# Graph step and expert layer on one core: weighted edge rows split into two fp32r parts, and nine node groups computed ahead instead of seven

## The chip, the cores and the metric

The kernel runs on one core of one Trainium2 chip. The metric is device time of one launch in microseconds (us), the median of several executions; less is better. The core has five engines with a queue each: TensorE (PE), VectorE (DVE), ScalarE (ACT), GpSimd (POOL) and SyncE (SP).

## The reference, cut to what matters

```python
def gnn(X, src, dst, w, W, b):                      # 12500 nodes x 256, 200000 edges, dst sorted
    support = X @ W
    return segment_sum(support[src] * w[:, None], dst, 12500) + b

def ffn(x, ...):                                    # 8 experts, 256 -> 512 -> 256
    rw = softmax(softmax(mean(x) @ Wr + br) * scale)        # one routing for all nodes
    top_w, top_i = top_k(rw, 2); top_w = softmax(top_w)
    y = sum(top_w[k] * (gelu(x @ W1[top_i[k]] + b1) @ W2[top_i[k]] + b2) for k in (0, 1))
    return layernorm(y + x) * gamma + beta

x = x + gnn(layernorm(x), src, dst, edge_weight, W, b)
x = x + ffn(layernorm(x))
```

The two experts are known only when the mean over all nodes is known, that is after the whole graph step.

## The kernel before, in words

**Data.** Nodes lie in 98 tiles of 128 (NT), which stand in 25 groups of four (NG, GT). Edges lie in 1564 columns of 128 (NE), called slots here; they are worked off backwards, so that the first node tiles have about 8 slots each and the last one 158.

**Opening, about 145 us.** Tables are built that say where each node tile ends in the list of slots. Each node row times its 1/deviation is written to `xr_d`. The first 96 slots (FRESH) are gathered from `x` itself, and VectorE works out their weights.

**Edge stage, to about 1994 us.** For each slot GpSimd issues an indirect DMA (line 513) that gathers 128 rows of 256 into `G`, a ring of 64 (RING). VectorE makes a weighted one-hot `OH` (line 969; ring of 8, OHR): 1 times the edge weight where the edge's destination is the row of the node tile. TensorE adds `OH.T @ G` into PSUM bank 0 (`edge`, line 1255), in fp32. After every second slot `event` (line 1257) looks whether something is due. What is due stands in an order written at build time by `events()` and turned into slot numbers on the chip:

- END: a node tile is complete. `chores` (line 1205: transposes, the product with W, more transposes, for this tile and those before it) and then `begin` (line 1221), which starts the next tile with the two slots that may hold edges of both tiles, matched by `OHX`. ScalarE does the `section` (line 652) of the tile: `copy`, `across`, `x1_row`, `pre`, `square`, `match` for the tile after the next, `root`, `turned`, `normal`.
- UPS, BOTH, DOWNS: a unit of expert work. The first 7 groups (AHEAD) go through all 8 experts before the routing is known, in fp32: `unit_up` (line 1227) and `unit_down` (line 1237). These are 56 units (UNITS); their results go to `y_d`. A BOTH event is the down products of one unit and the up products of the next. `events()` spreads them from tile 18 on by `room`, a weight per tile worked out from its slots.

**Post stage, from about 2010 us.** The routing is worked out. Then for each of the 18 groups that were not computed ahead (`post`) TensorE runs the two chosen experts as three fp32r products each (high x high, low x high, high x low): eight steps of `up` (line 1302) and `down` (line 1319), where step i of `up` for group k+1 stands before step i of `down` for group k. VectorE goes through one iteration per k: eight times `low_h` (line 1084, the low part of the hidden rows), and between them `total` and `give` (lines 1086, 1117: the sum, the layer norm) of group k-2, `low` (line 1050) of group k+1, and, if k-2 is in `pre_of`, `total` and `give` of one group computed ahead as well. `pre_of` = {1 + (len(post) - 3) * a // AHEAD}: with 7 groups ahead that is k-2 in 1, 3, 5, 7, 9, 11, 13, every second iteration. GpSimd adds beta to each group's rows (line 524), B2 to those of a group computed ahead (line 522), and works out the 1/deviation (line 529). SyncE's queue holds, in the order of the groups: the load of `YL` three groups on, a wait until the group is finished (`s_fin`), its store, the next loads. So the load behind a group computed ahead waits until that one is finished:

```python
            for n, g in enumerate(order):
                m = len(tiles(g))
                if g >= AHEAD:
                    if k + 3 < len(post):
                        load_yl(k + 3)
                    k += 1
                e.wait_ge(s_fin, 4 * n + m)
```

ScalarE makes the high part `YTh` from `YL` in `high` (line 747), in step 3 of the iteration before the one that uses it, and the activations of `hidden` (lines 794, 797) stand behind it in its queue.

Of the kernel before, what the change touches and what calls it, by code (L numbers as in the profile page):

```python
# [4 lines left out]
P = 128  # L5
NODES, D, F, E = 12500, 256, 512, 8
# [6 lines left out]
RING, GS, OHR = 64, 16, 8  # L13
# [8 lines left out]
AHEAD = 7  # L22
# [52 lines left out]
assert 2 * NEV <= 512  # L75


def gnn_ffn(nc, x, dflat, srct, dstt, wt, W, b, Wr, br, W1, b1t, W2, b2, gamma, beta, cst, iota_e, evt, out):
# [13 lines left out]
    with ctx:  # L92
# [14 lines left out]
        g_bc, be_bc, B2 = sb("g_bc", [P, D]), sb("be_bc", [P, D]), sb("B2", [P, D])  # L107
# [15 lines left out]
        b1s, b2s = sb("b1s", [P, 2, 4]), sb("b2s", [P, 2, D])  # L123
# [6 lines left out]
        ARENA = 49152  # L130
# [20 lines left out]
        G, OH = early("G", [P, RING, D]), early("OH", [P, OHR, P])  # L151
        Wsb = early("Wsb", [P, 2, D])
        BB, Bh, Bl, b2r = early("BB", [P, D]), early("Bh", [P, D], f32r), early("Bl", [P, D], f32r), early("b2r", [P, D], f32r)
        OHX, OHT = early("OHX", [P, 2, P]), early("OHT", [P, 2, 2, P])
# [10 lines left out]
        YE = early("YE", [P, 2, GT * D])  # L165
        XS = At(w_at)("XS", [P, XBUF, GT, D])
        Gf = G[:, :, :].rearrange("p r d -> p (r d)")

# [26 lines left out]
        W1A = At(4 * ARENA - 4 * E * 2 * F)("W1A", [P, E, 2, F])  # L195
# [11 lines left out]
        assert late.at - 4 * HID * GT * P <= 4 * ARENA - 4 * E * 2 * F  # L207
        YP = At(w2s_at)("YP0", [P, 2, GT, D]), late("YP1", [P, 2, GT, D])
        Z = late("Z", [P, 3, GT, D])

# [16 lines left out]
        s_bn, s_aggr, s_pow, s_oh = sem("dve_bn"), sem("dve_aggr"), sem("dve_pow"), sem("dve_oh")  # L227
# [94 lines left out]
        def _(e):  # L322
# [100 lines left out]
            e.dma_start(g_bc[:, :], row(gamma).to_broadcast([P, D])).then_inc(gb_in, 16)  # L423
            e.dma_start(be_bc[:, :], row(beta).to_broadcast([P, D])).then_inc(gb_in, 16)
# [24 lines left out]
            for k in range(2):  # L449
                e.dma_start(W2s[:, k, :, :], W2[bass.ds(chosen[k], 1), :, :].rearrange("o (c p) n -> p (o c) n", p=P)).then_inc(w2s_in[k], 16)  # L450
                e.dma_start(b2s[:, k, :], b2[bass.ds(chosen[k], 1), :].to_broadcast([P, D])).then_inc(b2_in, 16)
# [38 lines left out]
        def _(e):  # L490
# [25 lines left out]
            def add_rows(n):  # L516
# [7 lines left out]
                e.tensor_tensor(out=XL[:, n % 4, 0:m, :], in0=XL[:, n % 4, 0:m, :], in1=be_bc[:, :].unsqueeze(1).to_broadcast([P, m, D]), op=ALU.add).then_inc(s_xp, 1)  # L524
# [15 lines left out]
        def _(e):  # L540
# [25 lines left out]
            def match(t):  # L566
# [4 lines left out]
                for k in range(2):  # L571
                    step(e.activation(OHT[:, 0, k, :], iota, ACT.Abs, bias=XND[:, k:k + 1]))
# [814 lines left out]
```

## Time and profile before

| | |
|---|---|
| median of 3 runs | 2444.71 us (2444.54 to 2446.91) |
| profiled execution | 2445.58 us, its span 2443.8 us |
| opening | to about 145 us |
| edge stage | 145 us to about 1994 us |
| post stage | from about 2010 us to the end |
| granted TensorE clock, mean | 0.974 of full speed |
| PE, DVE, ACT, POOL busy | 90%, 42%, 48%, 66% of the span |

The span is the profiled execution from its first to its last instruction; 1.8 us of that execution lie around it. Instructions of an engine can overlap in the records, so a busy sum is a union of their times. A matmul in fp32 leaves two records, one in fp32r one. "issue" in a row means that the engine waited for nothing that the profile shows.

### The profile page before, as it was taken

The numbers are of one execution on the slowest core, as the hardware profiler recorded it, in microseconds if no ns is written. First come the engines' busy times: TensorE is split into PE (matmuls) and PEld (weight loads), VectorE is DVE, ScalarE is ACT, GpSimd is POOL, SyncE is SP. The second block draws the span as 40 slices with busy tenths as digits, with TensorE's granted clock in tenths as the row PEclk, the third lists the DMA queues.
The fourth block names the chain that finished last, engine by engine and source line by source line (L and its number), as shares of the span: only waits on it lengthen the run. The fifth ranks groups of instructions, "written<-read, shape, count | busy, mean of one in ns | idle before, by whom it ended". The sixth has DMA issues, their size and how long they took to land. (4 is left out here: it accounts for less than half of the span.)

```text
span 2443.8 us, 40837 instructions
## 1 busy us (share of the span) xinstructions
PE 2208.0 (90%) x9811; PEld 1699.2 (70%) x9812; DVE 1027.4 (42%) x2961; ACT 1171.2 (48%) x3171; POOL 1614.2 (66%) x1625
## 2 busy tenths in 40 slices
PE   2388899999999989999999999999999989999998
PEld 1266666676766766666677676777667767998897
DVE  7793323232322232222223223223222226789897
ACT  3477766665655554444434332232232126565663
POOL 6677777777777777777777777777777731323331
PEclk9799999999999999999999999999999989999999
DMA  9955565556755655555565565655565542333321
GB/s 343 326 167 165 154 178 173 176 173 183 242 179 174 179 178 175 174 176 180 149 192 175 180 180 157 197 180 172 160 182 182 181 131 93 106 104 118 125 70 65
DMA packets 237361, 414.93 MB, mean 170 GB/s; under 512 B 36243, under 2 KB 154822, under 8 KB 237224
## 3 DMA queue, kind: packets, MB, share of 16 engines
q0 software_dynamic: 75072, 205.10, 28.4%
q1 hardware_dynamic: 161720, 206.10, 26.2%
q10 hardware_dynamic: 432, 2.40, 0.3%
q14 instruction: 111, 0.91, 0.1%
q8 instruction: 26, 0.43, 0.1%
HBM read 332.81 MB, written 80.65 MB: 169 GB/s over the span
## 5 line engine op out<-in xcount | busy, mean ns | idle before, releaser
L513 POOL DMA_INDIRECT G<-xr_d,SRC x1468 | 1392.8, 949 | 447.2 <-issue 295.1
L969 DVE TENSOR_SCALAR OH<-CST,DL,WR 128x128 f32<-128x128 f32 x1564 | 565.7, 367 | 1281.6 <-PE ps L1255 937.2
L1255 PE MATMUL ps<-G,OH 128*128 x3128 | 745.4, 391 | 101.1 <-DVE OH L969 73.1
L1255 PEld LDWEIGHTS ps<-G,OH 128*128 128x128 f32 x3128 | 595.2, 194 | 262.0 <-issue 185.8
L1245 PE MATMUL ps<-W2u,H 128*128 128x256 f32 x1792 | 408.5, 387 | 20.2 <-issue 19.3
L1245 PEld LDWEIGHTS ps<-W2u,H 128*128 128x128 f32 x1792 | 342.2, 193 | 84.5 <-issue 38.3
L1234 PE MATMUL ps<-YU,W1u 128*128 128x512 f32 x896 | 394.0, 592 | 1.5 <-issue 1.1
L705 ACT ACTIVATE YE<-ps 128x512 f32<-128x512 f32 x112 | 66.8, 596 | 497.2 <-PE ps L1245 497.2
L1234 PEld LDWEIGHTS ps<-YU,W1u 128*128 128x128 f32 x896 | 170.1, 190 | 192.6 <-issue 183.7
L698 ACT ACTIVATE H<-ps,b1a 128x512 f32<-128x512 f32 x224 | 153.8, 687 | 208.0 <-PE ps L1234 207.8
L585 ACT ACTIVATE OHX<-OHT,WR 128x128 f32<-128x128 f32 x194 | 67.6, 394 | 237.7 <-PE ps L1255 237.4
L1084 DVE TENSOR_TENSOR Hlo<-Ht,Hhi 128x512 fp32r<-128x512 f32 (+1 forms) x144 | 135.0, 949 | 67.7 <-ACT Hhi L797 67.4
L1333 PE MATMUL ps<-W2h,Hlo 128*128 128x256 f32 x560 | 158.4, 283 | 0.0
L1333 PE MATMUL ps<-W2l,Hhi 128*128 128x256 f32 x560 | 158.4, 283 | 0.0
L1333 PE MATMUL ps<-W2h,Hhi 128*128 128x256 f32 x560 | 157.8, 282 | 0.0
L794 ACT ACTIVATE Ht<-ps,b1s 128x512 f32<-128x512 f32 (+1 forms) x144 | 97.7, 678 | 120.5 <-PE ps L1316 120.5
L529 POOL TENSOR_TENSOR ZR<-ZV,mhalf 128x4 f32<-128x4 f32 (+1 forms) x25 | 33.2, 1329 | 182.6 <-DVE ZV L1115 182.6
L513 POOL DMA_INDIRECT G<-in_x,SRC x96 | 92.8, 967 | 51.4 <-issue 23.8
L524 POOL TENSOR_TENSOR XL<-XL,be_bc 128x1024 f32<-128x1024 f32 (+1 forms) x25 | 65.3, 2623 | 86.5 <-ACT XN L755 86.5
L1213 PE MATMUL ps<-Wsb,AT 128*128 128x256 f32 x424 | 113.2, 391 | 0.2 <-ACTq L672 0.2
L1333 PEld LDWEIGHTS ps<-W2h,Hhi 128*128 128x128 f32 x560 | 106.9, 191 | 5.6
L1333 PEld LDWEIGHTS ps<-W2l,Hhi 128*128 128x128 f32 x560 | 106.9, 191 | 5.0
(176 smaller groups left out, 2391.6 us busy)
## 6 DMA issues: line engine op xcount, KB each, us to landing
W1u<-in_W SPq DMA_DIRECT2D x56, 512.0 KB, 3.9
W2u<-in_W SPq DMA_DIRECT2D x56, 512.0 KB
y_d<-YE SPq DMA_DIRECT2D x56, 512.0 KB, 5.4
G<-xr_d,SRC POOLq DMA_INDIRECT x1468, 2.8
x_d<-X SPq DMA_DIRECT2D x98, 128.0 KB
yt_d<-YT SPq DMA_DIRECT2D x98, 128.0 KB, 2.3
XR<-in_x SPq DMA_DIRECT2D x97, 128.0 KB
XS<-in_x SPq DMA_DIRECT2D x24, 512.0 KB, 12.4
```

The lines of the kernel that those rows point to most:

```text
L513: e.indirect_dma_start(out=G[:, s % RING, :], out_offset=None, in_=x if s < FRESH else xr_d, in_offset=bass.IndirectOffsetOnAxis(ap=SRC[:, ...
L585: e.activation(OHX[:, k, :], OHT[:, 1, k, :], ACT.Copy, scale=WR[:, bass.ds(odd + k, 1)]).then_inc(s_ohx, 1)
L698: e.activation(H[:, i, :], ps[:, UP[i % 2], :], ACT.Gelu, bias=b1a[:, u % E, i:i + 1]).then_inc(s_gelu, 1)
L705: e.activation(YE[:, u % 2, p * 2 * D:(p + 1) * 2 * D], ps[:, DN[p], :], ACT.Copy).then_inc(s_ye, 1)
L794: e.activation(Ht[:, i % HB, 0:w], ps[:, 4 + i % HB, 0:w], ACT.Gelu, bias=b1s[:, i // 4, i % 4:i % 4 + 1]).then_inc(s_ht, 1)
L969: e.tensor_scalar(OH[:, s % OHR, :], iota, DL[:, s:s + 1], WR[:, s + 1:s + 2], ALU.is_equal, ALU.mult).then_inc(s_oh, 1)
L1084: e.tensor_tensor(out=Hlo[:, h, 0:w], in0=Ht[:, i % HB, 0:w], in1=Hhi[:, h, 0:w].bitcast(f32), op=ALU.subtract).then_inc(s_hlo, 1)
L1213: e.matmul(ps[:, XB, 0:D], AT[:, c * P:(c + 1) * P], Wsb[:, c, :], start=False, stop=True, skip_group_check=True)
L1234: ins = e.matmul(ps[:, UP[i % 2], :], W1u[:, c, i * P:(i + 1) * P], YU[:, c, :], start=(c == 0), stop=(c == 1))
L1245: ins = e.matmul(ps[:, DN[p], h * D:(h + 1) * D], H[:, i, j * P:(j + 1) * P], W2u[:, i, :], start=(h == 0 and i == 0), stop=(i == 3), skip ...
L1255: e.matmul(ps[:, 0, 0:D], OH[:, r, :], Gf[:, bass.ds(g + r * D, D)], start=False, stop=True, skip_group_check=True).then_inc(s_main, 1)
L1333: ins = e.matmul(acc, hp[:, h, rows], wp[:, x_, f, :], start=(i == 0 and q % 2 == 0 and a == 0), stop=False, skip_group_check=True)
```

## The change

For every slot from the 96th on VectorE now does three operations instead of one. It writes the weighted rows rounded to fp32r into a new ring `XHI` (16 deep, SPR), an unweighted one-hot in fp32r (`pure(k)`; 16 places: the old `OH` and a new `OHQ`), and the rest of the weighted rows, in place over the gathered rows (`XLO`). TensorE adds two fp32r products of the one-hot, with `XHI` and `XLO`, in place of the fp32 product. `begin` for such slots is four fp32r products. The loop over slots has a body of 16 slots instead of 8. AHEAD goes from 7 to 9: 72 units instead of 56, 16 post groups instead of 18, and `pre_of` becomes k-2 in 1, 2, 3, 5, 6, 8, 9, 11, 12. The weight of a tile in `room` changes. `match` moves to the end of a section and waits for `begin`, since `begin` now reads what it writes. VectorE waits for the stores of `xr_d` before its first split, and SyncE for the last edge before it loads gamma and beta (their place in SBUF is now shared with `OHQ`).

```diff
-RING, GS, OHR = 64, 16, 8
+RING, GS, OHR, SPR = 64, 16, 8, 16
-AHEAD = 7
+AHEAD = 9
...
-    room = [max(0.0, 0.75 * slots[t] - 3.5) if t >= 18 else 0.0 for t in range(NT)]
+    room = [max(0.0, slots[t] - 3.0) if t >= 18 else 0.0 for t in range(NT)]
...
+        XHI = early("XHI", [P, SPR, D], f32r)
+        ROWS, OHQ = At(TOP)("ROWS", [P, 4, D]), At(TOP)("OHQ", [P, SPR - OHR, P], f32r)
+        OHP = At(oh_at)("OHP", [P, OHR, P], f32r)
+        XLO = At(g_at)("XLO", [P, RING, D], f32r)
+        def pure(k):
+            return OHP[:, k, :] if k < OHR else OHQ[:, k - OHR, :]
...
+            e.wait_ge(s_main, NE)
+            e.dma_start(g_bc, row(gamma).to_broadcast([P, D])).then_inc(gb_in, 16)
...
# in match, then in section
+                if t >= 2:
+                    e.wait_ge(s_begin, t - 1)
+                step(e.activation(OHB[:, :, :], OHA[:, :, :], ACT.Relu, bias=ones[:, 0:1], scale=-1.0))
...
-                if s["copy"] is not None and s["copy"] + 2 < NT:
-                    e.wait_ge(s_ohx, 2 * s["copy"] + 2)
-                    match(s["copy"] + 2)
                 if s["root"] is not None:
...
+                if s["copy"] is not None and s["copy"] + 2 < NT:
+                    e.wait_ge(s_ohx, 2 * s["copy"] + 2)
+                    match(s["copy"] + 2)
...
# VectorE
-            for s in range(FRESH - 8, NE):
+            for s in range(FRESH - 8, FRESH):
                 one_hot(s)
+            def split(s):
+                k, n = s % SPR, s - FRESH
+                e.wait_ge(gat[s % GS], 16 * (s // GS + 1))
+                e.wait_ge(s_main, s - SPR + 3 if n >= SPR else s - OHR + 1)
+                e.tensor_scalar(XHI[:, k, :], G[:, s % RING, :], WR[:, s + 1:s + 2], None, ALU.mult).then_inc(s_split, 1)
+                e.tensor_scalar(pure(k), iota, DL[:, s:s + 1], None, ALU.is_equal).then_inc(s_split, 1)
+                e.wait_ge(s_split, 3 * n + 1)
+                e.scalar_tensor_tensor(out=XLO[:, s % RING, :], in0=G[:, s % RING, :], scalar=WR[:, s + 1:s + 2],
+                                       in1=XHI[:, k, :].bitcast(f32), op0=ALU.mult, op1=ALU.subtract).then_inc(s_split, 1)
+            for l, lot in enumerate(lots):
+                e.wait_ge(xs_st[l], 16 * (len(lot) + (lot[-1] == NG - 1)))
+            for s in range(FRESH, NE):
+                split(s)
...
# TensorE
+            def edge_split(g, r):
+                e.matmul(ps[:, 0, 0:D], pure(r), XHI[:, r, :], start=False, stop=False, skip_group_check=True)
+                e.matmul(ps[:, 0, 0:D], pure(r), XLOf[:, bass.ds(g + r * D, D)], start=False, stop=True, skip_group_check=True).then_inc(s_main, 1)
...
+                for r in range(n):
+                    if r % 4 == 0:
+                        e.wait_ge(s_split, done + 3 * (r + 4))
+                    edge_split(g, r)
+                    if r % 2 == 1:
+                        event(a, r, g, False)
```

## Rows read from the trace of the kernel before

**Rows 1.** The page: busy time of each engine, its share of the span, instructions.
```profile
PE 2208.0 (90%) x9811; PEld 1699.2 (70%) x9812; DVE 1027.4 (42%) x2961; ACT 1171.2 (48%) x3171; POOL 1614.2 (66%) x1625
```

**Rows 2.** Busy time by engine, one quiet stretch of the edge stage.
```profile
core 0: us, PE busy (x) PEld busy (x) DVE busy (x) ACT busy (x) POOL busy (x), PEclk, DMA share, GB/s
1300.00:1500.00 200.00, 193.35 (x757) 140.09 (x756) 58.02 (x161) 75.17 (x197) 151.27 (x161) 0.99 0.60 182
```

**Rows 3.** The gathers, 145 to 1985 us: count, ns min/median/max, first and last start.
```profile
L513 POOL DMA_INDIRECT G<-xr_d,SRC x1468: 942/946/1027, 145.0 to 1983.8; - x184
...
DMA to landing us min/median/max: 2.6/2.8/6.3
```

**Rows 4.** GpSimd and VectorE in order of time, one stretch, and a stretched gather.
```profile
1010.56 0.95 POOL L513 DMA_INDIRECT G<-xr_d,SRC  x1 [0.30 <-PE ps L1255]
1011.04 0.52 DVE L969 TENSOR_SCALAR OH<-CST,DL,WR 128x128 f32<-128x128 f32 x1 [1.11 <-DMA G<-xr_d,SRC]
...
1011.81 0.95 POOL L513 DMA_INDIRECT G<-xr_d,SRC  x1 [0.30 <-issue]
...
1978.68 0.99 POOL L513 DMA_INDIRECT G<-xr_d,SRC  x1 [0.30 <-PE ps L1255]
```

**Rows 5.** TensorE in order of time: a unit, then the end of the edges.
```profile
1011.14 7.17 PE L1245 MATMUL ps<-W2u,H 128*128 128x256 f32 x32 [0.81 <-issue]
1018.14 7.03 PE L1234 MATMUL ps<-YU,W1u 128*128 128x512 f32 x16
...
1986.98 7.07 PE L1255 MATMUL ps<-G,OH 128*128 x32
1993.89 0.38 PE L1209 MATMUL ps<-CST,AS 128*128 128x128 f32 x2
...
1995.31 0.38 PE L1209 MATMUL ps<-CST,AS 128*128 128x128 f32 x2
```

**Rows 6.** The chain that ended last, one step of the post stage.
```profile
2040.11 1.43 PE ps L1333 x12
...
2042.93 1.43 PE ps L1333 x12
```

**Rows 7.** VectorE, durations: a scaled 256-wide row, a two-input one, the one-hots.
```profile
L915 DVE TENSOR_SCALAR BB<-Bl,CST x1: 353/353/353, 40.3 to 40.3; 128x256 f32<-128x256 f32 x1
L917 DVE SCALAR_TENSOR_TENSOR b2r<-Bh,CST,BB x1: 485/485/485, 40.6 to 40.6; 128x256 fp32r<-128x256 f32 x1
L969 DVE TENSOR_SCALAR OH<-CST,DL,WR x1564: 322/347/587, 72.9 to 1990.7; 128x128 f32<-128x128 f32 x196
```

**Rows 8.** VectorE in order of time, one post iteration (it begins at 2253.45).
```profile
2253.45 0.67 DVE L1084 TENSOR_TENSOR Hlo<-Ht,Hhi 128x512 fp32r<-128x512 f32 x1
...
2266.07 0.69 DVE L1084 TENSOR_TENSOR Hlo<-Ht,Hhi 128x512 fp32r<-128x512 f32 x1 [5.28 <-ACT Hhi L797]
...
2270.33 2.62 DVE L1084 TENSOR_TENSOR Hlo<-Ht,Hhi 128x512 fp32r<-128x512 f32 x1 [0.18 <-ACT Hhi L797]
2273.44 5.14 DVE L1084 TENSOR_TENSOR Hlo<-Ht,Hhi 128x512 fp32r<-128x512 f32 x2 [0.49 <-ACT Hhi L797]
```

**Rows 9.** Busy time by engine (columns of Rows 2), two post iterations of VectorE.
```profile
2227.80:2253.40 25.60, 25.60 (x165) 23.26 (x164) 25.39 (x57) 14.35 (x25) 7.55 (x4) 1.00 0.14 42
2253.40:2275.70 22.30, 20.72 (x131) 18.45 (x130) 16.32 (x33) 13.24 (x24) 9.02 (x4) 1.00 0.56 190
```

**Rows 10.** VectorE in order of time, where the third iteration begins, and the last low part.
```profile
2084.63 0.79 DVE L1084 TENSOR_TENSOR Hlo<-Ht,Hhi 128x512 fp32r<-128x512 f32 x1 [2.02 <-ACT Hhi L797]
...
2424.77 0.44 DVE L1084 TENSOR_TENSOR Hlo<-Ht,Hhi 128x256 fp32r<-128x256 f32 x1 [1.73 <-ACT Hhi L797]
```

**Rows 11.** GpSimd in order of time, then a piece of the chain that ended last.
```profile
2268.07 4.33 POOL L522 TENSOR_TENSOR XN<-XN,B 128x1024 f32<-128x1024 f32 x1 [8.60 <-ACT XN L755]
2272.36 5.68 POOL L524 TENSOR_TENSOR XL<-XL,be_bc 128x1024 f32<-128x1024 f32 x2
...
2256.04 7.67 DMA YL<-yt_d
```

More of the change, by code:

```diff
@@ L422, in _ @@
                         e.dma_start(br_sb[:, :], row(br)).then_inc(r_in, 16)
-            e.dma_start(g_bc[:, :], row(gamma).to_broadcast([P, D])).then_inc(gb_in, 16)
-            e.dma_start(be_bc[:, :], row(beta).to_broadcast([P, D])).then_inc(gb_in, 16)
+            e.wait_ge(s_main, NE)
+            e.dma_start(g_bc, row(gamma).to_broadcast([P, D])).then_inc(gb_in, 16)
+            e.dma_start(be_bc, row(beta).to_broadcast([P, D])).then_inc(gb_in, 16)
             for v in range(FINAL, FINAL + 3):
@@ L523, in add_rows @@
                 e.wait_ge(gb_in, 32)
[L524 removed]
+                e.tensor_tensor(out=XL[:, n % 4, 0:m, :], in0=XL[:, n % 4, 0:m, :], in1=ROWS[:, 1:2, :].to_broadcast([P, m, D]), op=ALU.add).then_inc(s_xp, 1)
             def rstd(n):
@@ L1225, in begin, with begin_split @@
                 e.matmul(ps[:, 0, 0:D], OHX[:, 1, :], Gf[:, bass.ds(g + D, D)], start=False, stop=True, skip_group_check=True).then_inc(s_begin, 1)
+            def begin_split(v, g, r):
+                e.wait_ge(s_ohx, v * 2 + 2)
+                e.wait_ge(s_as, v + 2)
+                for k in range(2):
+                    e.matmul(ps[:, 0, 0:D], OHB[:, k, :], XHI[:, r - 1 + k, :], start=(k == 0), stop=False, skip_group_check=True)
+                    ins = e.matmul(ps[:, 0, 0:D], OHB[:, k, :], XLOf[:, bass.ds(g + (r - 1 + k) * D, D)], start=False, stop=(k == 1), skip_group_check=True)
+                ins.then_inc(s_begin, 1)
             def unit_up(u):
@@ L1266, in event @@
                         with e.If(now == END):
-                            begin(v, g + (r - 1) * D)
+                            if fresh:
+                                begin(v, g + (r - 1) * D)
+                            else:
+                                begin_split(v, g, r)
                         e.reg_add(v_r, v_r, 1)
@@ L1275, in event @@
                     e.reg_mov(rel, e.snap(due) - a)
-            def slots(a, g, n):
-                for r in range(n):
+            with e.Fori(0, FRESH // OHR) as i:
+                a = e.snap(i * OHR)
+                g = e.snap((i & (RING // OHR - 1)) * (OHR * D))
+                e.reg_mov(rel, e.snap(due) - a)
+                for r in range(OHR):
                     if r % 4 == 0:
@@ L1282, in slots @@
                     if r % 2 == 1:
-                        event(a, r, g)
-            with e.Fori(0, NE // OHR) as i:
-                a = e.snap(i * OHR)
-                g = e.snap((i & (RING // OHR - 1)) * (OHR * D))
+                        event(a, r, g, True)
+            def slots(a, g, n, done):
                 e.reg_mov(rel, e.snap(due) - a)
-                slots(a, g, OHR)
-            a = NE // OHR * OHR
-            e.reg_mov(rel, e.snap(due) - a)
-            slots(a, a % RING * D, NE % OHR)
+                for r in range(n):
[4 more added lines that the diff above has]
+                        event(a, r, g, False)
+            laps = (NE - FRESH) // SPR
+            with e.Fori(0, laps) as i:
+                a = e.snap(i * SPR + FRESH)
+                g = e.snap((i + FRESH // SPR & RING // SPR - 1) * (SPR * D))
+                slots(a, g, SPR, e.snap(i * (3 * SPR)))
+            a = FRESH + laps * SPR
+            slots(a, a % RING * D, NE - a, 3 * SPR * laps)
             for v in range(FINAL, FINAL + 5):
```

53 lines of the change are left out of this document (29 added, 24 removed).

## The prediction

> **What bounds the kernel now.** I read the page first. TensorE is busy 90% of the span and VectorE 42% [rows 1], so one would say that TensorE is the bound and that cheaper edge products pay everywhere. The stretch in the middle of the edge stage says something else [rows 2]: TensorE is busy 193 of 200 us, and beside it GpSimd runs 161 operations, the last one cut by the window: one per 1.25 us. The gathers' own row [rows 3] has 1468 of them from 145.0 to 1983.8 us: 1838.8 / 1467 = 1.2535 us each. In order of time [rows 4] one takes 0.95 us, then 0.30 us pass, then the next one starts, whatever is named in the brackets. That is GpSimd's own pace: no gather waits for a buffer there. So the edge stage is bound by the issue of gathers, with TensorE just below it. TensorE comes to the same from below: 1564 edge products of 0.43 us (16 in 1986.98 to 1993.89, [rows 5]) are 675 us, 56 units of 7.17 + 7.03 = 14.2 us are 795 us, 97 ends of a tile of 1.42 us chores and 0.86 us begin (two such products) are 221 us. The sum is 1691 of 1849 us.
>
> The post stage is read from the chain [rows 6]: a step of up and down takes 2.82 us, a group of eight steps with its last product 23.0 us, and these steps follow each other almost without a gap, so there TensorE sets the pace. VectorE stands close behind it.
>
> **The edge stage, part by part.** An fp32r product of 256 columns takes 1.43 / 12 = 0.119 us [rows 6], so a split edge costs 0.24 us in place of 0.43, and begin 0.48 in place of 0.86. TensorE after the change: 96 x 0.43 + 1468 x 0.24 + 72 x 14.2 + 97 x 1.9 = 41 + 352 + 1022 + 184 = 1599 us. That is less than now, so the 16 units more (227 us) fit under the gathers, and the saving on the edges is spent on them. The gathers stay 1468 at 1.25 us: I expect nothing from the edge products themselves. In the last node tile (158 slots, 198 us of gathers) there are ten units: 142 + 38 + 2 = 182 us, which still fits.
>
> VectorE per slot: the scaled row as line 915, 0.353 us; the rest as line 917, 0.485 us; the one-hot at most 0.347 us [rows 7]. Together 1.19 us, under 1.25, and this is an upper bound, since neighbouring records overlap and the one-hot reads one scalar less. The lower bound is the widest of them, 0.485, if the others hid wholly behind it. Neither end reaches the gathers' pace, but 1.19 is near it, and I take 1.1. The wait on its own semaphore has the one-hot between, so it costs nothing. Ring `XHI` lets VectorE run 13 slots ahead of TensorE, 16 us, and a BOTH event is 14.2 us, so VectorE needn't stop in one.
>
> Where VectorE and GpSimd meet: a one-hot that starts 0.48 us after a gather takes 0.52 us and not 0.35 [rows 4], and the longest 0.587 [rows 7]. So VectorE waits for GpSimd, by at most 0.24 us. The other way round, a gather is stretched from 0.95 to 0.99 us in some bursts of one-hots [rows 4]; none of the 1468 exceeds 1.027 us [rows 3]. 1.2535 against 1.25 us is 5 us in all today. After the change two one-input operations stand beside each gather in place of one; I take 1 us more for this, between nothing and 0.04 x 1468 = 59 us.
>
> The Trainium skill has a rule that speaks against this change ("SBUF — State Buffer", section "SBUF: two separate sides"): while VectorE runs an operation that uses both of its ports, such as an fp32 copy within SBUF, GpSimd is locked out of the shared ports and "cannot write the descriptors". By it the gathers would slow; the time is that of the second rival below. The trace agrees only in part: the waits that it shows are nearly all on VectorE's side.
>
> The end of the edges: now the last gather starts at 1983.8 us [rows 3] and the edges end at 1993.9 [rows 5], since a down unit and 16 products stood in the way. After it: the last unit stands 14 slots before the end and is over in time, so 1983.8 + 2.8 landing [rows 3] + 1.2 split + 4 x 0.24 = 1988.8: **5 us saved**.
>
> Costs that I put at nothing: `match` later in ScalarE's queue (behind it stands the next tile's `copy`, 8 slots or 10 us later, and ScalarE is busy 75 of 200 us [rows 2]); VectorE's and SyncE's new waits (GpSimd has passed the same one at 145 us; gamma and beta are first used in the post stage, and what stands behind them in SyncE's queue, the last tiles' stores, is due only after the last edge anyway); 24 MB more of weights and results (the DMA share is 0.60, [rows 2]); tiles that hold more units early (TensorE's load is under the gathers' in every stretch of ten tiles, 83 to 89% by the same sum).
>
> **The post stage.** Two groups less are 2 x 23.0 = 46 us of TensorE. But the nine groups computed ahead now share 13 iterations. VectorE's iterations are these [rows 9]: with a group computed ahead 25.6 us, busy throughout; the next one, without, 22.3 us, with a wait of 5.3 us for ScalarE [rows 8]. That wait has its cause in the iteration before: `YL` is loaded only when the group computed ahead is finished, takes 7.7 us [rows 11], and lands about 10 us into the iteration, where ScalarE needs it for step 3. Today a long and a short iteration alternate: 47.9 or 46.6 us for two, near TensorE's 46. After the change two or three long ones stand together, and 25.6 us each is over 23.
>
> More than that: GpSimd's add of B2 (4.33 us) and its adds of beta (2.85 us each) [rows 11] hold VectorE up: `low_h` takes 2.62 us, and then 5.14 us for two, in place of 0.67 each while they run [rows 8]. These adds fall in the short iteration today. Where the next group computed ahead follows at once, they fall in a long one. The price is at least the stall of 2.62 - 0.67 = 1.9 us, when VectorE came late to it after a gap, and at most the whole add less one operation, 4.33 - 0.67 = 3.7 us. I take 2.4, near the row, so such an iteration takes 28.0 us.
>
> The sum from the third iteration on (it begins at 2084.6 [rows 10], and nothing before it changes): long with an add at 3, 4, 7, 10, 13 (28.0 each), long without at 5, 8, 11, 14 (25.6 each), short at 6, 9, 12 (22 each): 140 + 102.4 + 66 = 308.4. The 15th and last, of the half group, begins at 2393.0; with 0.5 us for each late `YL` within a long one, 2395.5. Its last low part then comes after 9.6 us (today's 15.5 us less the 5.5 us of waits) to 13 us: 2406.5. Today it comes at 2424.8 [rows 10]. So **18 us saved**, not 46: VectorE becomes the bound of this stage.
>
> **Sum.** 5 + 18 - 1 = 22 us. The profiled execution takes 2445.58 us, 1.8 around its span of 2443.8; it becomes 2423.6. The median of the runs is 0.9 below it: 2444.7 - 22 = 2422.7, rounded to **2422.5 us**.
>
> **The rivals.**
> *VectorE keeps up in the post stage.* For it: its lag behind TensorE can grow by some us before TensorE feels it, and over 13 iterations the work is about equal (nine of 25.6 and the others of 17 without their waits). Against it: the rows of 25.6 us have no gap. It gives 46 + 5: 2394 us.
> *Gathers are stretched (the other side).* VectorE's two one-input operations meet GpSimd's access to SBUF. If each gather were stretched as the one of 0.99 us: +59 us, 2422.5 + 58 = 2480 us. If each waited for the whole of an operation that it meets at random: (0.353² + 0.347²) / (2 x 1.25) = 0.098 us each, 144 us, 2566 us. It decides from 0.015 us per gather on (22 / 1468). Against it: rows 3 and 4.
> *VectorE is over 1.25 us per slot.* 1.19 us plus the wait of up to 0.24 us beside GpSimd is 1.43 us at the worst; then 1468 x 0.18 = 264 us slower. From 1.27 us on the kernel is slower. Against it: the records overlap.
> *The edge products don't get cheaper.* At 0.43 us an edge TensorE has 1599 + 279 = 1878 us of work for 1849 us: 145 + 1878 = 2023 us in place of 1994, so 29 - 18 = 11 us slower, 2456 us. Against it: rows 6 are the same kind of product.
>
> **How the numbers follow.** The forecast 0.60 (its own range 2410 to 2434: the add's 1.9 to 3.7 us in five iterations, the last iteration's 9.6 to 13, gathers up to 5 us more). VectorE keeps up 0.14. Gathers stretched 0.12, a third of it below the point where it decides. VectorE over 1.25 us 0.07. Products not cheaper 0.03. Something else, as often up as down, 0.04. The range 2391 to 2446 takes in the first two and the small cases of the others; some 0.17 are left out. Faster by over 0.2% (what a measurement of this kernel can tell from no change) 0.80, within 0.2% 0.05, slower 0.15.
>
> **What would show it.** In the profile after: gathers still 1.25 us apart and the last one starting near 1984 us; edges over near 1989; TensorE busy some 86% of the edge stage and VectorE some 85%; long iterations of VectorE of 25.6 to 29 us next to each other, no gaps in them, and TensorE with gaps in the post stage. It is wrong if gathers are 1.27 us or more apart, if VectorE is busy all the edge stage, or if the post groups still follow at 23.0 us.

## The result and the profile after

The changed kernel takes 2578.87 us (median of four, 2568.49 to 2579.63), the kernel before beside it 2445.12 us: 1.0536 times as long [1.0508, 1.0563]. The forecast was 2422.5 us, its range 2391 to 2446. It missed by 156 us, on the other side of no change.

The page and the quiet stretch, of the kernel after (columns as in [rows 1, 2]):

```profile
PE 2196.8 (85%) x10287; PEld 1669.2 (65%) x10288; DVE 1784.8 (69%) x5885; ACT 1211.1 (47%) x3231; POOL 1660.2 (64%) x1627
...
1300.00:1500.00 200.00, 180.87 (x808) 131.22 (x807) 139.16 (x472) 82.36 (x219) 152.78 (x156) 0.98 0.61 184
```

TensorE is less busy than before and the kernel is longer. In these 200 us GpSimd issues 155 gathers and a bit, not 160. The gathers of the whole stage, and what they waited for:

```profile
L531 POOL DMA_INDIRECT G<-xr_d,SRC x1468: 942/947/1241, 145.9 to 2065.9; - x184
...
its engine sat idle before it (us, times) until:
  issue: 366.3, 1202
  PE ps L1299: 131.9, 316
```

The median is [rows 3]'s within 1 ns, but the longest grew from 1027 to 1241 ns, and the last gather starts 82 us later than before: they start 1.309 us apart on average, over the 1.27 us that the prediction had named as a sign of being wrong. "PE ps L1299" is an edge product, but the line by itself doesn't show a wait: most of these 316 gaps are the 0.3 us that stand between any two gathers. Before the change the same line read:

```profile
  PE ps L1255: 156.2, 474
```

What shows it are the distances between two starts. 17 of them exceed 1.6 us now (longest 5.8 us), none did before: there gathers wait for room in their ring of 64, 36 us in all. The rest of the delay, some 46 us, is gathers that take longer. Between the last gather and the end of the edges stood 10 us before and 67 us now. Both say that TensorE falls behind the gathers. The end of the edges in order of time (here and below the record of a product lasts longer than its place in the pipe, so starts are what is to be compared):

```profile
2131.04 0.58 PE L1299 MATMUL ps<-XLO,OHQ 128*128 128x256 f32 x1 [2.53 <-issue]
...
2132.34 0.41 PE L1299 MATMUL ps<-XLO,OHQ 128*128 128x256 f32 x1
2135.14 0.66 PE L1241 MATMUL ps<-CST,AS 128*128 128x128 f32 x2 [2.39 <-issue]
```

The edges end at 2132.75 us, before at 1994.1. So everything up to there is 138.7 us longer and all the rest 443.7 us instead of 449.7, 6.0 us shorter: 138.7 - 6.0 = 132.7, the difference of the spans (2576.5 and 2443.8).

Where TensorE stands idle in the edge stage, first after (300 to 2127 us), then before (300 to 1990 us): waiting line, releaser, us in total, times, longest.

```profile
PE ps L1285 <- issue: 86.4, 71, 1.7
PE ps L1241 <- issue: 48.5, 61, 1.3
PE ps L1298 <- DVE XLO L1031: 26.0, 35, 2.0
PE ps L1263 <- ACT AS L607: 13.0, 6, 2.2
PE ps L1298 <- DVE XHI L1028: 6.4, 10, 1.0
PE ps L1298 <- DVE OHP L1029: 5.3, 10, 0.6
```

```profile
PE ps L1255 <- DVE OH L969: 30.6, 28, 3.1
PE ps L1245 <- issue: 19.3, 34, 1.1
PE ps L1255 <- issue: 19.0, 30, 1.0
```

"issue" is waiting for nothing that the profile shows: the time that TensorE's own instruction stream needs for loads, comparisons and branches. Before each unit (L1285) it is 1.2 us, 71 times; before chores (L1241) 0.8 us, 61 times. Before the change 34 units waited, 0.6 us each. And between edges, where no wait is named:

```profile
1713.27 0.28 PE L1298 MATMUL ps<-XHI,OHP 128*128 128x256 f32 x1
1713.39 0.28 PE L1299 MATMUL ps<-XLO,OHP 128*128 x1
1713.55 0.39 PE L1298 MATMUL ps<-XHI,OHP 128*128 128x256 f32 x1
1713.78 0.28 PE L1299 MATMUL ps<-XLO,OHP 128*128 x1
1713.90 0.28 PE L1298 MATMUL ps<-XHI,OHP 128*128 128x256 f32 x1
1714.02 0.28 PE L1299 MATMUL ps<-XLO,OHP 128*128 x1
1714.27 0.39 PE L1298 MATMUL ps<-XHI,OHP 128*128 128x256 f32 x1
```

Four products should start 0.12 us apart, a pair of slots every 0.48 us. The pair that begins at 1713.55 lasts until 1714.27: 0.72 us. Every second slot ends in `event`'s look at `rel`. I sorted the records from 300 to 2127 us by pair, without those that a unit or chores stand in: of 535 pairs 159 take about 0.48 us, and the mean is 0.73 us. It isn't the clock: 516 of them ran wholly at the full granted clock, and their mean is 0.72 us.

VectorE is idle, too, and for TensorE: the whole stage's waits of it are one line.

```profile
DVE XHI L1028 <- PE ps L1299: 614.9, 78, 15.0
```

So the ring of 16 does stop VectorE, up to 15 us at a time. From this I had two theories. **S**: TensorE's sequencer, the part of the engine that works through loads, comparisons and branches and hands products on, is the bound, as the short products no longer cover its time. **R**: the two engines stop for each other at each unit. A third, **G**, was the second rival of the prediction: gathers are stretched by VectorE.

### The profile page after: what moved, and what is told of

The parts are those of the page before. It is cut to its first block and busy times, and to the rows that moved or that the text cites. A ratio compares the mean times of both kernels' runs of the same rounds, so it can differ in the third digit from the quotient of the medians.

```text
span 2576.5 us, 45199 instructions
## 1 busy us (share of the span) xinstructions
PE 2196.8 (85%) x10287; PEld 1669.2 (65%) x10288; DVE 1784.8 (69%) x5885; ACT 1211.1 (47%) x3231; POOL 1660.2 (64%) x1627
## 5 line engine op out<-in xcount | busy, mean ns | idle before, releaser
L1028 DVE TENSOR_SCALAR XHI<-G,WR 128x256 fp32r<-128x256 f32 x1468 | 526.2, 358 | 644.6 <-PE ps L1299 637.2
L1031 DVE SCALAR_TENSOR_TENSOR XLO<-G,WR,XHI 128x256 fp32r<-128x256 f32 x1468 | 697.7, 475 | 0.0
L1285 PE MATMUL ps<-W2u,H 128*128 128x256 f32 x2304 | 551.9, 401 | 87.6 <-issue 87.6
L1285 PEld LDWEIGHTS ps<-W2u,H 128*128 128x128 f32 x2304 | 456.9, 201 | 169.0 <-issue 102.5
L1298 PE MATMUL ps<-XHI,OHP 128*128 128x256 f32 x736 | 232.9, 338 | 40.7 <-DVE XLO L1031 21.9
L1298 PE MATMUL ps<-XHI,OHQ 128*128 128x256 f32 x732 | 225.7, 334 | 13.3 <-DVE XLO L1031 8.4
L1029 DVE TENSOR_SCALAR OHP<-CST,DL 128x128 fp32r<-128x128 f32 x736 | 213.0, 289 | 0.0
L1029 DVE TENSOR_SCALAR OHQ<-CST,DL 128x128 fp32r<-128x128 f32 x732 | 211.4, 289 | 0.0
L1299 PE MATMUL ps<-XLO,OHP 128*128 (+1 forms) x736 | 200.0, 298 | 0.0
L1298 PEld LDWEIGHTS ps<-XHI,OHP 128*128 128x128 f32 x736 | 144.8, 197 | 78.9 <-DVE XLO L1031 32.9
L1299 PE MATMUL ps<-XLO,OHQ 128*128 x732 | 191.3, 288 | 2.5 <-issue 2.5
L1299 PEld LDWEIGHTS ps<-XLO,OHP 128*128 128x128 f32 x736 | 144.8, 197 | 17.4 <-issue 14.4
L1299 PEld LDWEIGHTS ps<-XLO,OHQ 128*128 128x128 f32 x732 | 142.8, 195 | 10.9 <-issue 10.9
```

The costliest lines, as they stand in the source:

```text
L1028: e.tensor_scalar(XHI[:, k, :], G[:, s % RING, :], WR[:, s + 1:s + 2], None, ALU.mult).then_inc(s_split, 1)
L1029: e.tensor_scalar(pure(k), iota, DL[:, s:s + 1], None, ALU.is_equal).then_inc(s_split, 1)
L1031: e.scalar_tensor_tensor(out=XLO[:, s % RING, :], in0=G[:, s % RING, :], scalar=WR[:, s + 1:s + 2], in1=XHI[:, k, :].bitcast(f32), op0=ALU ...
L1285: ins = e.matmul(ps[:, DN[p], h * D:(h + 1) * D], H[:, i, j * P:(j + 1) * P], W2u[:, i, :], start=(h == 0 and i == 0), stop=(i == 3), skip ...
L1298: e.matmul(ps[:, 0, 0:D], pure(r), XHI[:, r, :], start=False, stop=False, skip_group_check=True)
L1299: e.matmul(ps[:, 0, 0:D], pure(r), XLOf[:, bass.ds(g + r * D, D)], start=False, stop=True, skip_group_check=True).then_inc(s_main, 1)
```

## The experiments

### One part alone: 7 groups with the split, 9 groups without it

`a7` is the changed kernel with one number set back, `b9` the kernel before with it set forward.

```diff
-AHEAD = 9        # a7, in the changed kernel
+AHEAD = 7
-AHEAD = 7        # b9, in the kernel before
+AHEAD = 9
```

> The changed kernel with 7 groups computed ahead as before. Theory S (TensorE is the bound of the edge stage, because its short products no longer cover what its sequencer does between them: 0.36 us per slot instead of 0.24, 1.2 us before each unit, 0.6 us before each chores): 16 units less are 16 x (14.2 + 1.2) = 246 us less, TensorE's 1987 us become some 1740, under the gathers' 1849; the edges end at 1990 to 2000 us and the kernel takes 2430 to 2450 us. Theory R (VectorE and TensorE stop for each other at each unit, because VectorE can be only 13 slots ahead): 56 such stops in place of 72, the 138 us of loss become some 107, about 2550 us. Theory G (gathers are stretched by VectorE's operations): the number of units has no part in it, 2490 to 2580 us.

> The kernel before with 9 groups computed ahead, nothing else changed. TensorE then has 1691 + 227 = 1918 us of work in the edge stage plus the some 90 us that it stood idle: edges end at 2135 to 2160 us, the kernel at 2580 to 2610 us. Theory S: about as slow as the changed kernel or 10 to 40 us slower, since the split products saved only part of their 0.19 us per slot. Theories R and G: the changed kernel's loss has its cause in the split, not in the units; TensorE's own sum then still says that this one is slower than before by at least 1918 - 1849 = 69 us (2515 us).

`a7`: 2488.0 us, 1.0171 [1.0154, 1.0188], outside the ranges of all three theories (G's began at 2490). `b9`: 2596.8 us, 1.0617 [1.0599, 1.0635], as expected by S. The gathers of `a7`, then of `b9`:

```profile
L531 POOL DMA_INDIRECT G<-xr_d,SRC x1468: 942/946/1228, 143.2 to 2025.8; - x184
```

```profile
L513 POOL DMA_INDIRECT G<-xr_d,SRC x1468: 942/946/1028, 144.6 to 2081.7; - x184
```

In `b9` the edges end at 2154 us. The 16 units more cost 160 us in the edge stage by themselves (16 x 14.2 = 227 less what idle time took in), and the split gives back only 21 us of it (2154.2 - 2132.8). The shorter products did save something: counted from 145 us on, a pair takes 0.90 us in `b9` and 0.74 in the changed kernel, which is 117 us for 734 pairs. But before units and chores TensorE now waits 135 us for its own instruction stream, in `b9` 23, and that takes 112 us back.

In `a7` TensorE is not the bound: VectorE waits for gathers most of the time, 324 us for them against 153 for TensorE.

```profile
DVE XHI L1028 <- DMA G<-xr_d,SRC: 323.7, 540, 12.0
DVE XHI L1028 <- PE ps L1299: 152.5, 35, 12.5
```

The edges of `a7` end at 2032.5 us, 38 us later than before, and the last gather starts 42 us later, although no gather waited for a full ring long enough to show (no distance between two starts exceeds 1.6 us). Over 1.251 us each, the distances add up to 47 us, before to 4 us. So G holds as well: 44 us. S expected 2430 to 2450 us here and left that out.

### Doubling the suspected cost

```diff
                     e.reg_mov(rel, e.snap(due) - a)
+                with e.While(lambda: e.snap(rel) <= r - 64):
+                    e.reg_add(rel, rel, 64)
```

> The changed kernel with a second, never fulfilled comparison and branch of TensorE's sequencer after each of those that look for the next event (every second slot); no work is added. One costs the sequencer 0.25 to 0.3 us. Theory S: 734 pairs of slots x 0.2 to 0.3 us = 140 to 210 us more, 2720 to 2790 us. Theory R: TensorE's pace between units is VectorE's, 0.86 us per slot; only the first 13 slots after a unit count, 0.14 x 13 x 72 = 130 us at most, and as VectorE goes on meanwhile some 40 to 60 us. Theory G: nothing, within 0.5%.

> The kernel before with the same second comparison and branch. Its pair of slots takes 0.86 us of products, the sequencer's own time for a pair is 0.62 to 0.66 us, with the second check 0.9 to 0.95. Theory S: 782 pairs x 0.05 to 0.1 = 40 to 80 us more of TensorE's time, of which the gathers' pace hides a part: 0 to 60 us slower, far less than the changed kernel loses by the same. Theories R and G: nothing.

After the change: 2840.2 us (1.1611 [1.1586, 1.1637]), 261 us more than without it, 261 / 734 = 0.36 us for a pair of slots, fully paid and more than the 140 to 210 us expected. (The 48 pairs of the opening have the extra look too; the first gather from `xr_d` starts no later for it.) A part of it is the clock: the granted clock of the edge stage fell from 0.96 to 0.92; the pairs that ran at full clock grew from 0.72 to 1.01 us, by 0.29. Before: 2557.5 us, 112 us more (1.0459 [1.0442, 1.0477]), 0.15 us for a pair. The direction is that of S, the sizes are not: I had expected 0 to 60 us before. R has no place for a loss of 261 us.

The trace has the sequencer's own instructions as well (PEldq), which the busy times leave out. In the changed kernel, 300 to 2100 us, the look at `rel` and the registers for the address of a low part:

```profile
L1302 PEldq COMPARE_BRANCH  x970: 69/201/221, 307.3 to 2096.7; - x194
L1302 PEldq MOVE  x821: 29/29/29, 307.5 to 2096.6; - x165
L1299 PEldq FUSED_REGOPS  x1344: 46/46/56, 307.9 to 2096.4; - x192
```

The distance between the starts of two such comparisons, with no event between them, is the sequencer's own time for a pair; it hardly varies (medians, us):

| kernel | plain pair | with a wait for VectorE | with the loop's end | mean of a loop body | products of a pair |
|---|---|---|---|---|---|
| before | 0.60 | 0.73 | 1.31 | 0.81 | 0.86 |
| changed | 0.62 | 0.75 | 1.55 | 0.79 | 0.48 |
| `check2_after` | 0.99 | 1.08 | 1.89 | 1.14 | 0.48 |
| `hi_only_c`, below | 0.37 | 0.47 | 1.11 | 0.50 | 0.24 |

So the sequencer of the kernel before already needed 0.81 us for a pair, just under the 0.86 us of its products. Halving the products leaves a stream that is nearly as long as before. (That the measured mean is 0.73 us and not 0.79 fits a lead that the sequencer gains while a unit's products run; this is argued and not measured.) The second look adds 0.35 us to it, 257 us for 734 pairs, which is the loss of `check2_after`.

### Leaving out a product

```diff
-                e.matmul(..., pure(r), XHI[:, r, :], start=False, stop=False, ...)
-                e.matmul(..., pure(r), XLOf[:, bass.ds(g + r * D, D)], start=False, stop=True, ...).then_inc(s_main, 1)
+                e.matmul(..., pure(r), XHI[:, r, :], start=False, stop=True, ...).then_inc(s_main, 1)
```

> The changed kernel (9 groups ahead) without the product of the low part, a third time: the two earlier runs of it fell where transfers were slow and the kernel before took 3285 us. Beside a kernel before of 2445 us: theory S (TensorE's sequencer) edges end at 2030 to 2045 us and the kernel takes 2470 to 2490 us; theory R (hand-off ring, VectorE's pace) 2560 to 2580 us.

2506.5 us, 1.0239 [1.022, 1.0257]: 72 us less than the changed kernel. The edges end at 2054.9 us, 78 us earlier; S had 2030 to 2045, R 2115 to 2135, so S is missed by 10 us and R by 60. The last gather starts at 2035.9, and the gathers that take over 0.95 us add up to 52 us beyond it, so they have become the nearer bound. The kernel's time lies between the two ranges given for it (S 2470 to 2490 us, R 2560 to 2580). VectorE still stops for TensorE almost as long as before:

```profile
DVE XHI L1028 <- PE ps L1298: 538.4, 75, 15.1
```

That decides against R: 538 us in place of 615 in the stops that R holds to be the cause, and yet over half the loss of the edge stage is gone. By itself the run doesn't tell a product's time from that of the register instructions before it, since both go: per pair 0.24 us of products and, by the table, 0.25 us of the sequencer.

### The ring of 32 slots

```diff
-RING, GS, OHR, SPR = 64, 16, 8, 16
+RING, GS, OHR, SPR = 32, 16, 8, 32
```

`XHI` lies in the room that the gathers' ring gives up; TensorE's loop body has `SPR` slots.

> The changed kernel (9 groups ahead) with a hand-off ring of 32 slots in place of 16 between VectorE and TensorE (rows' high parts and one-hots), so that VectorE can be 29 slots ahead; for the room the gathers' ring has 32 slots instead of 64. TensorE's loop body has 32 slots instead of 16. Theory R (the two engines stop for each other at each unit): VectorE at 0.86 us per slot does 16 slots in a unit of 14.2 us and no longer stops, most of the 138 us of loss in the edge stage is gone, edges end at 2000 to 2045 us, kernel 2445 to 2490 us. Theory S (TensorE's sequencer): its time per slot and at each unit stays, only 46 of 92 ends of the loop body at some 0.7 us go: 2540 to 2580 us.

This run, and 12 more of the 18, fell on chips where the kernel before takes 3257 to 3288 us instead of 2445, so only ratios within one group of runs and single rows of them can be used. I put it down to slow transfers, in the expectations too; the profiles don't bear that out (a unit's result lands in 5.2 us there, in 5.5 otherwise). Only the opening and the edge stage are longer there: `hi_only`, on such a chip, and `hi_only_c` are the same kernel, their edges end at 3010.5 and 2054.9 us, and from there to the end they take 444.5 and 442.9 us. The cause stays open. The ring has three more runs:

> The changed kernel with the hand-off ring of 32 slots again (gathers' ring 32, loop body of 32 slots); in the first run of it the transfers were slow on the chip and the kernel before took 3285 us. Beside a kernel before of 2445 us: theory R 2445 to 2490 us, theory S 2540 to 2580 us.

> The ring of 32 slots a third time (the first two ran where transfers were slow and the kernel before took 3285 us). Beside a kernel before of 2445 us: theory R 2445 to 2490 us, theory S 2540 to 2580 us.

> The changed kernel with a hand-off ring of 32 slots, loop body of 32 slots, gathers' ring of 32. Without the low products the changed kernel just came to 2506 us, nearer theory S (2480) than R (2570). For the ring theory S says 2540 to 2580 us beside a kernel before of 2445; theory R 2445 to 2490 us; and if TensorE waits for VectorE by some 41 us in all, as the trace of the changed kernel shows, and nothing else changes, 2530 to 2550.

1.0908 [1.0842, 1.0974], 1.0913 [1.0871, 1.0954], 1.0957 [1.0933, 1.098] and 1.1003 [1.0968, 1.1038]. On such chips it is slower than `hi_only` (1.05) and `a8` (1.03); the changed kernel itself has no run on one, so what the ring does to it isn't measured. There is a reason of its own in the profile. First the queue that brings instructions (packets, MB, share of the DMA engines), then waits of TensorE, 300 to 3100 us, both of `ring32_d`:

```profile
q8 instruction: 569, 9.32, 1.2%
```

```profile
PE ps L1298 <- issue: 515.8, 252, 8.9
...
PE ps L1285 <- issue: 64.8, 73, 3.8
```

The changed kernel moves 0.51 MB on that queue. The loop body of 32 slots is fetched again and again, and TensorE waits 516 us at edges for no other engine. So the run doesn't measure the ring alone. One row is of use: VectorE waits for a product of TensorE once, 14.5 us, where it was 615 us, and TensorE's wait of 0.9 us before each unit is still there. A ring of 32 with a loop body of 16 wasn't tried.

### Which operation stretches the gathers

In `a7` 132 gathers take about 1.21 us. One of them, GpSimd, then VectorE beside it:

```profile
1055.51 1.21 POOL L531 DMA_INDIRECT G<-xr_d,SRC  x1 [0.30 <-PE ps L1299]
1057.03 0.95 POOL L531 DMA_INDIRECT G<-xr_d,SRC  x1 [0.31 <-issue]
...
1055.43 0.47 DVE L1031 SCALAR_TENSOR_TENSOR XLO<-G,WR,XHI 128x256 fp32r<-128x256 f32 x1
1055.83 0.34 DVE L1028 TENSOR_SCALAR XHI<-G,WR 128x256 fp32r<-128x256 f32 x1
1056.09 0.27 DVE L1029 TENSOR_SCALAR OHP<-CST,DL 128x128 fp32r<-128x128 f32 x1
```

I took the last two, one-input operations back to back, for the cause, and gave the high part a second input:

```diff
-                e.tensor_scalar(XHI[:, k, :], G[:, s % RING, :], WR[:, s + 1:s + 2], None, ALU.mult)
+                e.scalar_tensor_tensor(out=XHI[:, k, :], in0=G[:, s % RING, :], scalar=WR[:, s + 1:s + 2],
+                                       in1=ones[:, 0:1].to_broadcast([P, D]), op0=ALU.mult, op1=ALU.mult)
```

> The changed kernel with 7 groups ahead, and the high part computed by VectorE as (row x weight) x 1 with a second input, a column of ones, in place of the one-input scale; same values. The 7-group version's gathers lose 44 us: 132 of them take 1.21 us, each where a high part and a one-hot ran directly behind each other in the gather's time. Theory G (GpSimd is held up while VectorE runs one-input operations back to back): with the high part in a two-input form no such pair is left, the last gather starts at 1984 to 1995 us, edges end at 1990 to 2000, kernel 2440 to 2455 us. Its rival, that VectorE's traffic as such stretches them: VectorE's slot becomes 0.97 us in place of 0.86, the gathers lose as much or more, 2485 us or over.

> 7 groups ahead, the high part in a two-input form, again, beside an undisturbed kernel before. In the run with slow transfers its gathers were stretched more (165 us in all beyond 0.95 us each, against 44 to 55 us with the one-input form), so I now give the theory of one-input pairs less than half. By it: 2440 to 2455 us, last gather at 1984 to 1995. By its rival (VectorE's traffic as such): last gather at 2025 to 2150 us, kernel 2490 to 2610 us.

3216 us (0.9794 [0.9747, 0.9842]) and 3207 us (0.9761 [0.9731, 0.979]) beside 3285 and 3288. Here the kernels with 7 groups are faster than the kernel before, while `a7` on another chip is 1.7% slower: on these chips not even the sign of a ratio can be carried over. The gathers of `a7_stt_b`:

```profile
L531 POOL DMA_INDIRECT G<-xr_d,SRC x1468: 942/1023/1309, 193.2 to 2691.0; - x184
```

The median rose from 946 to 1023 ns; beyond 0.95 us each the gathers took 163 us more in all, in `a7` 47. The chip has a small part in this: the same sum is 53 and 71 us in `hi_only` and `hi_only_b`, and 52 in `hi_only_c`. That theory fell: two-input operations stretch them more, not less. Then the other way round, without any two-input operation in the stage:

```diff
-                e.wait_ge(s_split, 3 * n + 1)
-                e.scalar_tensor_tensor(out=XLO[:, s % RING, :], ...).then_inc(s_split, 1)
...
-                e.matmul(..., pure(r), XLOf[:, bass.ds(g + r * D, D)], ...)
+                e.matmul(..., pure(r), XHI[:, r, :], ...)
```

> The changed kernel with 7 groups ahead and VectorE's computation of the low part left out; the second product of each edge takes the high part once more (wrong sums, same work for TensorE). With 7 groups the gathers lost 44 us. If it is the two-input operation running when a gather starts that holds the gather up: last gather at 1984 to 1990 us, kernel 2443 to 2450 us. If it is one-input operations back to back (which are all that is left on VectorE): last gather at 2000 to 2030, kernel 2460 to 2490. If it is TensorE (theory S) that sets the 7-group kernel's time: 2485 us, with gathers no longer stretched but waiting for their ring.

> 7 groups ahead, VectorE's low part not computed (the second product of each edge takes the high part again). The 7-group kernel took 2488.0 us, its gathers were stretched by 44 us and the last one started at 2025.8 us. If the two-input operation that runs when a gather starts stretches it: last gather 1984 to 1990 us, kernel 2443 to 2450. If any running operation does, in proportion to its length (0.35 and 0.28 against 0.48 us): stretch of 15 to 30 us, last gather 2000 to 2015, kernel 2460 to 2475. If it is one-input operations back to back: 2480 to 2500.

3240.7 us (0.9868 [0.9843, 0.9893]) and 3208.6 us (0.9841 [0.9799, 0.9884]). (TensorE's work isn't the same, as the expectation has it: without the address registers its sequencer needs 0.37 us for a plain pair there and not 0.62.) By the same sum the gathers are stretched by 51 and 53 us, in most cases to 1.00 to 1.15 us (396 and 395 gathers) and none to the 1.21 us that 132 gathers of `a7` take (a few take 1.3 to 1.53 us). So each of VectorE's operations can hold a gather up, the longer ones for longer; how much each brings in the 44 us of `a7` isn't measured, as on these chips the gathers and VectorE meet at other moments.

### The post stage

`hi_nob2` is `hi_only` without GpSimd's add of B2.

```diff
-                    e.tensor_tensor(out=XN[:, n % 3, 0:m, :], ..., in1=B2[...], op=ALU.add).then_inc(s_xb, 1)
+                    e.sem_inc(s_xb, 1)
```

> The changed kernel without the product of the low part again (the output lacks it), beside an undisturbed kernel before: theory S 2470 to 2490 us with gathers still stretched by some 44 us, theory R 2560 to 2580 us.

> The changed kernel (9 groups ahead) with two things left out, one in each stage: the product of the low part for each edge slot from the 96th on, and GpSimd's add of B2 in the post stage (the output lacks both). Edge stage: theory S (TensorE's sequencer is the bound) edges end at 2030 to 2045 us instead of 2132.8, theory R (VectorE and TensorE stop for each other, 0.86 us per slot) 2115 to 2135. Post stage: if the add is what makes VectorE's long iterations 30 to 31 us instead of 25.5, five of them shrink by some 5 us, and from the end of the edges to the end 415 to 425 us are left of 443.7; if it is the late YL and ScalarE, 440 to 445.

Their edges end at 3003 and 3012 us, both on chips of the slower kind; their post stages can be compared, since VectorE's iterations in that of `hi_only_b` are those of the changed kernel within 0.8 us. Iterations 3 to 14 and then the tenth alone, of `hi_only_b`, and under it of `hi_nob2` (columns as in [rows 9]):

```profile
3099.60:3418.30 318.70, 291.67 (x1796) 261.65 (x1796) 275.29 (x597) 168.72 (x300) 107.19 (x50) 0.96 0.32 106
3285.00:3316.10 31.10, 31.10 (x201) 28.25 (x200) 26.41 (x57) 17.07 (x30) 12.64 (x6) 1.00 0.11 35
```

```profile
3108.50:3409.80 301.30, 286.89 (x1806) 258.17 (x1805) 259.19 (x598) 170.04 (x302) 85.41 (x41) 0.98 0.34 112
3286.60:3313.20 26.60, 26.60 (x170) 24.10 (x169) 23.49 (x58) 16.03 (x29) 7.96 (x4) 1.00 0.13 41
```

Without the add the twelve iterations take 17.4 us less: 4.4 to 4.6 us in each of the three with an add that follow a short iteration (7, 10 and 13), 2.2 and 0.9 us in the other two (3 and 4), the rest in between. The stage from the end of the edges on is 425.4 us for 444.0.

### Two more group counts

> The changed kernel with 8 groups ahead. Theory S: TensorE's edge stage is 1987 - 8 x 15.4 = 1864 us, less than the stretched gathers' 1849 + 44 = 1893, so still gather-bound or just so: edges end at 2035 to 2065 us; the post stage one group shorter, but with a part of it given back to VectorE as with 9: 6 to 15 us less. Kernel 2475 to 2505 us. Theory R: 64 stops for 72, 2530 us.

> The changed kernel with 8 groups ahead, ring of 32, loop body of 32 slots and the two-input form. Theory S: TensorE 1864 - 32 = 1832 us, just under the gathers. If the two-input form takes the stretch away: edges end near 1995, post stage 10 to 20 us shorter than before's, 2425 to 2440 us, faster than both. If it stretches gathers more: 2490 us or more, and then gathers are the bound.

`a8`: 1.0291 [1.0229, 1.0354], `a8_ring32_stt`: 1.0605 [1.0564, 1.0647], both beside a kernel before of some 3285 us. The second was meant to beat both kernels; its 32-slot loop body is fetched again like that of `ring32` (9.34 MB), and its gathers are stretched by 95 us. `hi_only` had a first run on such a chip, too:

> The changed kernel with the product of the low part left out for each edge slot from the 96th on (VectorE still computes the low part, the output lacks it). TensorE has two products and their register instructions less per pair of slots. Theory S: the pair falls from 0.62 to 0.66 us of the sequencer's time to some 0.4 us, 734 x 0.24 = 176 us less, TensorE falls below the gathers; what remains is the gathers' own stretch as with 7 groups ahead (last gather at 2025.8 us): edges end at 2030 to 2045 us, kernel 2470 to 2490 us. Theory R: both engines go at VectorE's 0.86 us per slot after each unit, whatever the product costs: 2560 to 2580 us.

1.0497 [1.0454, 1.0541], and `hi_only_b` 1.0489 [1.0458, 1.0521].

## Why the prediction was wrong

**What bounds the kernel now** was read rightly: the gathers' pace, TensorE just under it. `b9` confirms the sum of TensorE's work: 1691 + 227 = 1918 us, and measured are 2154.2 - 145 = 2009 us, of which TensorE's records leave 81 us idle.

**The step that failed** is "a split edge costs 0.24 us in place of 0.43", and with it the 1599 us "less than now, so the 16 units more fit under the gathers". Halving the products stayed right, and the sum took the time between them for nothing. The row of 0.119 us was right for the product and wrong for the slot: it comes from the post stage, whose chain has no branch between products. In the edge stage a comparison stands after every second slot, the loop's end after every 16th, and a chain of loads and branches before each unit; TensorE's sequencer needs 0.79 us for a pair of slots where the sum has 0.48. Measured were some 1987 us from the first gather to the last edge. The parts of the 388 us that were missing:

- pairs of slots at 0.73 us in place of 0.48: 734 x 0.25 = 184 us, with the short waits for VectorE (41 us) in it
- 1.2 us before each of 72 units and 0.8 us before most chores: 135 us, before the change 23 us
- units at 14.75 us in place of 14.2 (547.9 and 499.1 us for 71 of them): 40 us. Their down products mean 401 ns in the changed kernel, 387 before and 382 in `b9`. That is the clock: after a gap TensorE's records last longer for a while (0.58 and 0.66 us at 2131 to 2135 us, where the granted clock is 0.50, the lower of its two levels), and the mean granted clock fell from 0.974 to 0.948, with 0.979 in `b9`. The 52 units whose down products ran wholly at full clock take 0.219 us a product, as in `b9`; the other 20 take 0.277.

They add up to 359; 18 us more are waits for ScalarE, and 11 aren't assigned. `check2_after` and the sequencer's records show the first by experiment and row; the second and third rest on rows (with `b9` beside them, which has as many units, waits 23 us and has no longer units). The claim of the fourth rival, that edge products don't get cheaper, was near this, for another reason, and at 0.03 it was priced far too low.

**"VectorE needn't stop"** was wrong in its numbers: it takes 0.86 us per slot and not 1.1, so that it fills the 13 slots in 11 us and then stops, and it is busy 67% of the edge stage and not 85%. The price of that is small: TensorE waited 41 us for VectorE.

**Gathers stretched by 1 us more** was wrong by itself: with 7 groups, where it counts, it is 44 us, inside the bound of 0 to 59 us that I had given and above the 22 us from which that rival decides. In the changed kernel TensorE hides it. `a7` is 1.7% slower than the kernel before: the split loses even without the two groups.

**The end of the edges**: "5 us saved" had no chance with 67 us between the last gather and the last edge.

**The post stage** was the right mechanism: VectorE is the bound, no 46 us. Long iterations next to each other are there, 30.9 and 26.4 us:

```profile
2414.90:2445.80 30.90, 30.90 (x199) 28.06 (x198) 27.81 (x57) 17.21 (x31) 12.88 (x6) 1.00 0.11 35
2445.80:2472.20 26.40, 20.22 (x106) 17.29 (x105) 23.22 (x57) 10.63 (x19) 5.17 (x3) 0.81 0.42 140
2472.20:2494.40 22.20, 22.06 (x141) 19.70 (x140) 16.33 (x32) 14.07 (x26) 8.96 (x4) 1.00 0.56 190
```

Each window is one iteration of VectorE, the 10th, 11th and 12th. The twelve iterations took 319.9 us instead of 308.4. The five long ones with an add are 154.0 us instead of 140, and all others together 2.5 us shorter than forecast, so the term that was off is the long iteration with an add, 30.8 us on average and not 28.0. The add's price is a part of it: I took 2.4 us each, 12 in all, and leaving it out gave 17.4. Even without it these iterations take 26.6 to 29.5 us and not 25.6; why isn't shown. (A slip of no weight: today's last low part comes 15.1 us after its iteration begins, not 15.5; in the changed kernel it is 8.9.) From the third iteration to the end it is 348.1 us for 359.2 before, 11 us saved and not 18, and 5 us were lost between the edges and the third iteration; an "issue" gap of 2.4 us right behind the last edge is one part of that (the gap of 2.5 us lies before the last edges).

## What to carry to other kernels

A product's time in a straight chain is not its time in a loop with branches: before making products shorter, ask how long the engine's own instruction stream takes between them, and look for "issue" waits that already show at the places where the queue runs empty. The sequencer's own records tell it before anything is changed (here 0.81 us a pair, against 0.86 us of products), and doubling an empty branch in the kernel before tells it in one run. And before filling a freed engine with moved work, measure the two parts apart: here the moved work cost 160 us, and what was to pay for it brought 21.

## What the hardware showed unexpectedly

- A second comparison and branch of TensorE's sequencer cost 0.36 us a pair of slots where nothing covers it (0.35 us by the sequencer's records, 0.20 of them the comparison's own), and 0.15 us behind products of 0.86 us a pair.
- A loop body of 32 slots made the instruction queue move 9.32 MB in place of 0.51, with waits of up to 8.9 us at the edges in `ring32_d`, which ran on a chip of the slower kind; one of 16 slots didn't, on either kind.
- A gather is held up by VectorE's operations of either form: 0.95 us became 1.21 in 132 gathers of `a7` (1.23 at most), and the median 1.02 with a two-input high part. The Trainium skill ("SBUF — State Buffer", section "SBUF: two separate sides") says that VectorE and GpSimd share a pair of ports, which goes for a whole instruction to whichever starts first: GpSimd's, or a VectorE operation in a mode with two ports or, if GpSimd's reads SBUF, with two inputs there. The runs agree in that both forms hold gathers up and the longer one for longer; which mode VectorE was in no row shows. But most gathers in VectorE's full bursts still took 0.95 us; which moment of a gather is the sensitive one stays open.
